# Moving the third and fourth tile's look-ups into the F stage of an embedding-and-CIN kernel

## The reference

```python
e = jnp.stack([tbl_0[ids[:, 0]], ..., tbl_25[ids[:, 25]]], axis=1)          # 512 x 26 x 32
x1 = jnp.einsum('bik,bjk,hij->bhk', e, e, W1) + b1[None, :, None]           # h = 128
x2 = jnp.einsum('bik,bjk,hij->bhk', x1, e, W2) + b2[None, :, None]
z = jnp.sum(jnp.concatenate([x1, x2], axis=1), axis=-1)                     # 512 x 256
h = jnp.concatenate([z, dense_ctx], axis=1)
h = jnp.maximum(h @ W_top1 + b_top1, 0.0)
h = jnp.maximum(h @ W_top2 + b_top2, 0.0)
y = h @ W_top3
```

## Time and profile before

| | |
|---|---|
| median of 3 runs | 255.42 us (255.09 to 255.67) |
| the profiled execution | 255.76 us, its span 253.8 us |
| TensorE busy | 147.2 us, 58% of the span |
| VectorE, ScalarE, GpSimd busy | 107.4, 88.3, 85.4 us |
| mean granted clock of TensorE | 0.80 |

### The profile page before, as it was taken

The page is one execution under the profiler, slowest core; times in us unless marked ns, Lnnn a source line. Parts: engine busy times, 40 slices in busy tenths (PEclk is TensorE's granted clock), DMA queues, the critical chain, the costliest instruction groups (busy, mean ns, idle before and its releaser), DMA issues.

```text
span 253.8 us, 3289 instructions
## 1 busy us (share of the span) xinstructions
PE 147.2 (58%) x1169; PEld 129.5 (51%) x1169; DVE 107.4 (42%) x397; ACT 88.3 (35%) x295; POOL 85.4 (34%) x96
## 2 busy tenths in 40 slices
PE   0784001300003243020058999999999999999995
PEld 0772001000001131000034899998999899989994
DVE  6940019100000003000049998992589458945401
ACT  2540001000010401040037779857447744774112
POOL 3877777777777777771000000000000000000000
PEclk9999555555555586555558999999999999999999
DMA  6650000000010100000000020100000000000000
GB/s 193 230 109 13 13 14 14 13 13 13 13 13 14 18 13 13 13 13 5 0 0 0 0 87 0 21 0 4 0 15 7 3 0 15 6 0 3 12 9 2
DMA packets 7350, 5.86 MB, mean 23 GB/s; under 512 B 3473, under 2 KB 6805, under 8 KB 7206
## 3 DMA queue, kind: packets, MB, share of 16 engines
q1 hardware_dynamic: 4230, 3.86, 5.1%
q0 software_dynamic: 2816, 1.45, 3.9%
q10 hardware_dynamic: 288, 0.35, 0.5%
HBM read 5.18 MB, written 0.00 MB: 20 GB/s over the span
## 4 chain that ended last, share of the span: by engine, by line
PE 46%; another core or an unknown queue 29%; issue 12%; ACT 8%; DMA 3%; SPq 0%; ACTq 0%
PE p_zh L888 12%; PE p_t L868 12%; PE p_t L876 7%; DMA region<-in_L_rec_W 3%; ACT e_diag L325 3%; PE p_x L930 3%; PE p_t L843 2%; PE p_zh L843 2%; PE p_zh L896 2%; PE p_t L828 1%; ACT region L416 1%; PE p_x L888 1%; PE p_x L941 1%; PE p_t L960 1%
## 5 line engine op out<-in xcount | busy, mean ns | idle before, releaser
L303 POOL DMA_INDIRECT rows<-in_tbl,idx x88 | 84.5, 960 | 29.3 <-issue 26.5
L843 PE MATMUL p_zh<-S,region 128*128 128x352 f32 (+1 forms) x26 | 13.2, 641 | 54.6 <-issue 29.5
L843 PE MATMUL p_t<-S,region 128*128 128x352 f32 (+1 forms) x26 | 14.4, 682 | 40.9 <-ACT region L416 22.3
L630 DVE TENSOR_TENSOR region<-region 128x14 f32<-128x14 f32 (+10 forms) x11 | 2.9, 303 | 81.0 <-issue 51.1
L843 PEld LDWEIGHTS p_zh<-S,region 128*128 128x128 f32 x26 | 6.2, 257 | 60.7 <-issue 60.1
L843 PEld LDWEIGHTS p_t<-S,region 128*128 128x128 f32 x26 | 6.2, 262 | 47.5 <-issue 46.8
L888 PE MATMUL p_zh<-region 124*128 124x128 f32 x256 | 29.6, 277 | 0.0
L888 PEld LDWEIGHTS p_zh<-region 124*128 124x128 f32 x256 | 28.9, 192 | 0.5
L325 ACT COPY e_diag<-eT 32x160 f32<-32x160 f32 (+2 forms) x80 | 28.6, 358 | 0.8
L333 ACT COPY region<-p_t 124x352 f32<-124x352 f32 x32 | 14.5, 452 | 20.6 <-PE p_t L868 19.8
L760 DVE COPY L<-p_t 74x208 f32<-74x208 f32 x24 | 8.9, 371 | 22.8 <-PE p_t L876 22.8
(11 more groups left out here) (118 smaller groups left out, 249.8 us busy)
## 6 DMA issues: line engine op xcount, KB each, us to landing
region<-in_L_rec_W SPq DMA_DIRECT2D x1, 1664.0 KB
rows<-in_tbl,idx POOLq DMA_INDIRECT x88
wt<-in_W_top SPq DMA_DIRECT2D x1, 512.0 KB
region<-in_W_top SPq DMA_DIRECT2D x1, 512.0 KB
region<-in_tbl SPq DMA_DIRECT2D x4, 125.0 KB
w<-in_L_rec_W ACTq DMA_DIRECT2D x1, 338.0 KB, 3.3
gmix<-L SPq DMA_DIRECT2D x4, 56.0 KB
gmix<-L SPq DMA_DIRECT2D x4, 30.0 KB
```

Source lines behind the costliest of these rows:

```text
L303: pool.indirect_dma_start(rows[:, t, f * EMB:(f + 1) * EMB], None, tables[f], bass.IndirectOffsetOnAxis(ap=idx[:, t, f:f + 1], axis=0),).t ...
L843: last = nc.tensor.matmul(p_f[n % 2][:, j1 - 1 - j, 0:width], w2T[:, j, :], S[:, 0:width], start=True, stop=True)
```

## The change

It has four parts. `look_up(2)` moves from behind the F stage to behind slice 7, where it waits for the second `choose`; `look_up(3)` moves to behind slice 11. The banks change: the third tile's look-up goes into `p_w` (which the second tile's used) and the fourth's into `p_x`, so the transposes of the weights, which used `p_x`, now use `p_t[1][0]` and `p_t[0][1]`. `choose(1)` moves up on VectorE, from behind `group(0, 4)` to behind `high_pairs(20)`. VectorE evicts the weights' transposes before tile 1's first two transposes of rows, and `choose(3)` moves from before all that to between the two. The wait for all rows goes from before the dense part into `z_sums`.

```diff
-        p_wt = [p_t[0][0], p_w, p_x, p_t[1][0]]
-        p_over, p_rows = p_t[1] + [p_z2, p_h1], [p_x, p_w, p_x, p_h1]
+        p_wt = [p_t[0][0], p_w, p_t[1][0], p_t[0][1]]
+        p_over, p_rows = p_t[1] + [p_z2, p_h1], [p_x, p_w, p_w, p_x]
...
             for m in reversed(range(20, FIELDS - 1)):
                 high_pairs(m)
+            choose(1)
             group(0, 2)
...
             group(0, 3)
             group(0, 4)
-            choose(1)
             top_fields()
...
             choose(2)
-            choose(3)
             dve.wait_ge(small_in, 16 * SMALL)
...
+            for i in range(1, WT_BANKS, 2):
+                dve.wait_ge(wt_done, i + 1)
+                nc.vector.tensor_copy(WT[0:ROWS0, 4 * i:4 * i + 4, :],
+                                      p_wt[i % 4][0:ROWS0, :].rearrange("p (s h) -> p s h", h=P)).then_inc(wt_saved[1], 1)
+            choose(3)
             for t in range(1, TILES):
                 rows_to_columns(t, 0)
                 rows_to_columns(t, 1)
-                if t == 1:
-
-                    for i in range(1, WT_BANKS, 2):
-                        dve.wait_ge(wt_done, i + 1)
...
                 rows_to_columns(t, 2)
...
                     look_up(1)
-            pe.wait_ge(chosen_ready, 1)
-            look_up(2)
-            pe.wait_ge(f_saved, len(SLICES) - 1)
-            look_up(3)
+
+                if n == 7:
+                    pe.wait_ge(chosen_ready, 2)
+                    look_up(2)
+                if n == 11:
+                    look_up(3)
...
                          cleared=True).then_inc(z2_done, 1)
+                pe.wait_ge(rows_ready, TILES)
                 pe.wait_ge(mix_in[t], 16 * MOVES)
...
             for i in range(WT_BANKS):
+                if i == 3:
+                    pe.wait_ge(t_saved[0], TURNS)
                 if i >= 4:
...
-            pe.wait_ge(rows_ready, TILES)
             pe.wait_ge(top_in, 16 * 4)
```

More of the change, by code:

```diff
@@ L769, in _ @@
                 rows_to_columns(t, 1)
-                if t == 1:
-                    for i in range(1, WT_BANKS, 2):
-                        dve.wait_ge(wt_done, i + 1)
-                        nc.vector.tensor_copy(WT[0:ROWS0, 4 * i:4 * i + 4, :],
-                                              p_wt[i % 4][0:ROWS0, :].rearrange("p (s h) -> p s h", h=P)
-                                              ).then_inc(wt_saved[1], 1)
                 rows_to_columns(t, 2)
```

## The result

The changed kernel took **261.17 us** (median of 4 runs, 260.70 to 261.75), the kernel before 255.43 (255.09 to 255.67) beside it: the ratio is 1.0227 [1.0203, 1.0251]. It is slower, by 5.7 us where the forecast had 3.1, and ends 0.17 us above the forecast's range. The profiled execution took 261.28 (span 259.2, mean clock 0.788), against 255.76 (253.8, 0.798).

A forecast was written before the change was run, and what follows sets the result against it. Bound by an unnamed wait up to 128.84 us, then by TensorE with a few ScalarE links. Look-ups 2.6 plus VectorE's tail 0.5 make 3.1 us: from 255.42 to 258.5 us, range 257.2 to 261.0.

The forecast's parts named there:

- A rule weighed against the trace: TensorE's wait before the first turn becomes 3.4 us; the skill's 3 us rule says the clock would fall there.
- the hold: First case: the clock stays full over the gap before the first turn, 258.5 us, own range 257.8 to 259.3; chance 0.51.
- The rival with the fallen clock: Clock falls in the gap before the turns, which lose 1.7 to 2.4 us, say 2.0: 260.5 us; chance 0.29.
- The look-ups between the slices: Look-ups behind slices 7 and 11 start the first turn at 148.5 instead of 145.93: +2.6 us, bounds 1.79 and 3.58.
- ScalarE's new wait before slice 9's eviction: Sign in the changed profile: ScalarE's eviction of slice 9 follows a wait of over 1.5 us.
- VectorE's tail: Tile 1's VectorE work comes 2.7 us later, delaying `spread(1, 3)`, `save_h1(0)` and `h2_sums`: +0.5 us, bounds 0 and 0.8.
- `choose(1)` earlier, banks, waits: VectorE's small work held back until 128.8, new banks and moved waits: priced at nothing; one bank's stall would cost 0.4.
- The long wait: ScalarE's unnamed wait to evict slice 5, ending at 128.84; expected to stay, with slice 7 not moving.
- The rivals in which it ends an 11.9 us step sooner or later: Unnamed wait before slice 5's eviction shifts: sooner gives 251.4 us, chance 0.09; later gives 270.4, chance 0.06.
- the look-ups hide anyway: ScalarE's waits in the F stage (1.72, 0.73, 0.38) are room for the look-ups: time stays 255.4 us; chance 0.05.

The follow-up runs named there:

- a3_vector_back: Changed kernel with VectorE's evictions again behind tile 1's first two transposes and `choose(3)`: 260.71 us, ratio 1.0183 to the kernel before.
- a1_fill: Changed kernel with 12 unread products behind slice 14, and SyncE sending the second weight matrix only after the first turn: 260.83 us, ratio 1.0147 to the kernel before.
- e3_fill_vector_back: Changed kernel with 12 unread products behind slice 14 and VectorE's evictions in their old order, at the 153 us level: 154.78 us, ratio 1.0092 to the kernel before.
- a2_lookups_back: Changed kernel with both look-ups put back behind slice 14, the rest of the change kept: 258.25 us, ratio 1.0015 to the kernel before.
- a4_third_in_f: Changed kernel with `look_up(3)` put back behind slice 14, `look_up(2)` staying behind slice 7: 259.33 us, ratio 1.0125 to the kernel before.
- e2_fill: Changed kernel with 12 unread products (24 passes) behind slice 14, at the 153 us level: 155.30 us, ratio 1.0131 to the kernel before.
- e1_before: The kernel before, unchanged, timed and traced at the 153 us level: 153.31 us, ratio 0.9995.
- p1_pause: Kernel before, with GpSimd waiting for the evictions of all 15 slices before tile 1's gathers: 162.40 us, ratio 1.0582.
- c2_after: The changed kernel itself, run again on a third chip at the 153 us level: 157.50 us against 154.98, ratio 1.0146.
- d2_behind_ten: Kernel before with only `look_up(2)` moved behind slice 10, `look_up(3)` staying behind slice 14: 155.56 us, ratio 1.0010.
- b_gap: Kernel before with look-ups of tiles 2 and 3 cut to one product each, bank and two waits altered: 154.08 us, ratio 1.0060.
- e4_evict_first: Kernel before with `look_up(2)` behind slice 10, two spreads earlier, and VectorE's weight evictions ahead of tile 1's first two transposes: 152.72 us, ratio 0.9948.

## Why the prediction was wrong, point by point

**The step that failed** is the choice in "A rule weighed against the trace": that the clock holds over the new gap. The gap was forecast at 3.4 us and is 3.30. It lay between waits that the trace knew (0.56 without a fall, 3.8 and 5.2 with one), and I gave the hold 0.51 against 0.29. All four traces of kernels with this gap lost the clock (the changed kernel three times, `a3_vector_back` once), and ten of twelve executions by their mean clock; filled, it was kept in all ten, and in the trace of `a1_fill`. (`e3_fill_vector_back`, filled too, kept it in its four.) The cost was priced well: +1.70 in the turns, the lower end of 1.7 to 2.4, though that end came from 3.4 us at half, for which no row stood in the prediction. 3.4 us was 0.4 from a wait that had lost the clock and 2.5 from the longest that had kept it (0.93 at 18.22 in TensorE's timeline, not the 0.56 that I named); the odds should have followed that. The Trainium skill (TensorE: Matmul & The Clock Gate, section "Why this matters for your kernels") warns of gaps over about 3 us between bursts, and the traces agree with it at 3.30. They don't make it a safe line: below it the clock fell after 1.97, 1.98 and 2.24 us and held through 2.63, 2.88 and 2.96 (last section).

A second step failed with it, the top of the range. The rival with the fallen clock stood in it at 260.5, and its own bounds (257.8 to 259.3 and 1.7 to 2.4 more) reach 261.7; the range ended at 261.0. The measured 261.17 lies in what was left off. Against the rival's 5.1 us over the kernel before, the spans show 5.4: 0.5 more for the look-ups, 0.1 before slice 7, 0.3 less for the turns. The other 0.3 of the 5.7 is between the medians and not in the two traces.

**The look-ups between the slices** were right in mechanism. Measured +3.1 for 2.6. The 0.5 above is again the clock: the rise that the earlier trace rows put at 134.7 came at 135.8, so 1.1 us more ran at half. With a full clock the term is 2.68. I had taken the moment of the rise as fixed, and that is a weak step. It isn't the added work alone that moves it, though. `a2_lookups_back`, whose list there is the kernel before's, has the rise at 133.0 and not at 134.8; with one look-up between the slices (`a4_third_in_f`) it came at 134.0, with both at 135.8, 135.4 (`a3_vector_back`) and 136.1 (`a1_fill`). So it moves by up to 1.8 us, or 0.9 us of time, from one execution to another with the same work; with two look-ups all three were later than all others, and more can't be said from six traces. A smaller miss: I placed ScalarE's new wait before slice 9's eviction, and it is before slice 8's (4.44, then 0.21); the sum of the two is what was meant, 4.65 instead of 2.45. That each look-up has its own share, 1.79 and then about 0.9, fits `a4_third_in_f`, which leaves 1.6 to 1.7 for the first.

**VectorE's tail** was right: +0.50 in the trace of the case, gone again in that of `a3_vector_back`, and 0.52 by time in `e2_fill` against `e3_fill_vector_back`; forecast 0.5. `spread(1, 3)` waits 0.38 for VectorE in ScalarE's timeline, as described:

```profile
174.68 0.37 ACT L343 ACTIVATE z<-p_zh,bias_k 128x128 f32<-128x128 f32 x1 [0.38 <-PE p_zh L888]
176.03 1.42 ACT L325 COPY e_diag<-eT 32x160 f32<-32x160 f32 x4 [0.38 <-DVE eT L580]
```

**`choose(1)` earlier, banks, waits** at nothing: slice 7 starts 0.1 later, the stretch of the weights' transposes and everything behind `h2_sums` is unchanged to 0.1. No run tried them alone, but `a2_lookups_back` keeps them all at a ratio of 1.0015.

**The long wait** stayed: it ends at 128.8 to 128.9 in the kernel before, the changed one and the four variants at this level, whatever stood on VectorE or behind slice 7. The rivals in which it ends an 11.9 us step sooner or later are out. That the look-ups hide anyway is out too, by `a2_lookups_back`.

## What to carry to other kernels

Work moved out of the seam between two stages leaves an idle stretch there, and its price is not only what the moved work delays: if the stretch nears those which have cost the clock before, count the next microseconds at half speed, and let the range hold that case with all its own bounds. Don't treat the moment at which the clock rises as fixed either. An operation that looks cheap to hide inside a pipeline of two engines is hidden only where the engine that it blocks is not the one waited for; here the place behind slice 10 took one look-up almost for nothing, behind slices 7 and 11 two cost 2.7 us. If a gap can't be closed with useful work, filling it with products nobody reads was better here than leaving it empty.

## What the runs showed of the hardware

**The same program at 255 and at 153 us.** On some chips the engines that wait for TensorE go on tens of microseconds after its rows end, in the first half. Two lines of ScalarE's timeline in the kernel before, of the case; slice 4 was issued at 87.19 and slice 5 at 99.09, and the rows below are their evictions:

```profile
109.81 0.25 ACT L409 COPY region<-p_t 128x14 f32<-128x14 f32 x2 [10.87 <-remote]
...
128.82 0.26 ACT L409 COPY region<-p_zh 128x14 f32<-128x14 f32 x2 [16.29 <-remote]
```

In `e1_before`, at 153 us, TensorE is through the whole F stage at 38.8. GpSimd issues its gathers at about the same pace at both levels (the last ends at 115.5 in the kernel before of the case, at 119.2 in `e1_before`), so they alone aren't the cause. What is stays open: the one run meant to tell, `p1_pause`, fell on a chip without the lateness. The change costs 5.7 us at the one level and, by medians against the chip's own kernel before, 4.2 and 2.5 at the other.

**The clock may fall after the work has begun again.** In the case it was full throughout the idle 3.2 us and at half from 149.5, with TensorE busy; in `c2_after` it fell before the turn. Behind this gap the windows at half are 3.3 us long in the case and 6.6 in `c2_after`, and in two of twelve executions the mean clock was full: the spread of the changed kernel, 5 us where the kernel before has 0.3 on the same chip, is in large part this. What else sets the six longest 2.4 us apart is mostly open; between the two that were traced (160.35 and 158.70), 1.28 us lie before slice 7 (30.47 and 29.19), where the program is unchanged.

**The length of a wait alone doesn't decide.** In all traces, TensorE's waits of 1.5 to 1.8 us at the full clock kept it. From there to 3.4 us both happened: 1.91 (`a3_vector_back`), 1.95 (`p1_pause`), 2.00 (`a1_fill`), 2.63 (`d2_behind_ten`), 2.88 (`b_gap`) and 2.96 (`p1_pause`) kept it; 1.97 (`p1_pause`), 1.98 (`a4_third_in_f`, at 17.62), 2.24 (`e4_evict_first`) and the 3.30 of the change, in four traces of four, lost it. The same 16 products last 2.83 us behind a wait of 1.97 in `p1_pause` and 2.05 behind one of 2.63 in `d2_behind_ten`:

```profile
101.23 2.83 PE L932 MATMUL p_x<-region 128*128 128x128 f32 x16 [1.97 <-ACT region L356]
```

```profile
124.01 2.05 PE L931 MATMUL p_x<-region 128*128 128x128 f32 x16 [2.63 <-ACT region L354]
```

What else decides no run here shows.
